# Adding the intra-chunk numerator to the inter-chunk product on TensorE instead of VectorE, in a causal linear-attention and mixture-of-experts kernel

## The chip, the cores and the metric

The kernel runs on one core of a Trainium2 chip. The metric is the device time of one execution in microseconds (us), from launch to end; the span in the profile is the shorter stretch from the first to the last instruction. The engines are named as in the profile: PE is TensorE (PEld its weight loads), DVE is VectorE, ACT is ScalarE, POOL is GpSimd, SP is SyncE. SBUF is the on-chip working memory, PSUM the memory that PE writes its products to.

## The reference

One sequence of 2048 tokens of width 128 goes through causal linear attention (16 heads of 8), a residual and a layer norm, then a top-2 mixture of 8 experts, a residual and a second layer norm. The change lies in the attention, which is, cut to what matters:

```python
q = elu(x @ Wq.T) + 1;  k = elu(x @ Wk.T) + 1;  v = x @ Wv.T     # (l, 16, 8) each
kv_cumsum = cumsum(k[..., :, None] * v[..., None, :], axis=l)
k_cumsum  = cumsum(k, axis=l)
out = einsum('lhd,lhde->lhe', q, kv_cumsum)
normalizer = clip(einsum('lhd,lhd->lh', q, k_cumsum), 1e-6, None)
x = layernorm(x + (out / normalizer[..., None]).reshape(l, 128) @ Wo.T)
```

What follows (router, softmax, top 2, two gated matrix products per expert, weighted sum, layer norm) isn't touched by the change.

## The kernel before, in words

The tokens are 16 chunks of 128, in 4 groups of 4. A chunk n (n from 0 to 15) goes through these instructions in the attention stage:

- PE projects x to q, k, v (`project`, L547). ACT makes exp and relu of q and k and copies v (`inputs`, L770 to L774). DVE forms elu + 1 of q and k in one instruction with two SBUF inputs (`features`, L952, written to `qk`). POOL forms all products k times v, with a ninth column of ones per head for the normalizer, as one SBUF instruction of 128x1152 (`outer`, L455, written to `kv`).
- PE transposes q (L555) and forms the prefix sum over the chunk's tokens as three products with a triangular matrix, one per bank (`prefix`, L560, widths 432, 432 and 288). In this document they are called the first, second and third prefix sum of the chunk.
- DVE multiplies each of the three by q (L978) and sums over d (L985) to `num`, the chunk's own numerator and normalizer, 128x144. It masks the running state of all earlier chunks for the next chunk (`mask_state`, L963).
- PE multiplies the transposed q by the masked state (`inter`, L574) to `inter_ps` in PSUM. DVE adds `num` to `inter_ps` (L994), clips the normalizer columns (`den`, L997), takes the reciprocal (L1000) and multiplies (`o`, L1004).
- PE transposes o (`turn_o`, L581), updates the state (`state`, L567), and forms the output product and residual (`put_out`, L587, L589). ACT copies on the way.

Every engine has its own queue, written out in order by a `step(g, m, ...)` function that all engines run through in the same order (`groups`); chunk n = 4g + m. Engines meet only in semaphores. DVE's `attend(n)` (called step n below) does in this order: `features` of chunk n+3, the three products of chunk n, the sum L985, `mask_state` of chunk n+1, the addition L994, `den`, the reciprocal, `o`. PE does `project` of chunk n+4, `prefix` of chunk n, `turn_o` of chunk n-1, `state` of n, `inter` of n, `put_out` of n-1; the prefix sums of chunk n+1 wait only for their PSUM bank (`pre_used`), so PE can run a chunk ahead of DVE. POOL's `outer` of chunk n+3 waits for `features` of chunk n+3.

Between these, `between(i)` interleaves on DVE the layer-norm statistics and the routing of the group before, one kind of work per step of the group (`parts`, L1185): in steps 5, 9 and 13 the variance (`mean_and_variance`, with `negm` L1045 and `vare` L1053, L1060), in steps 6, 10 and 14 the shift (`shifts_of`, L1066, at i = 3), in steps 7, 11 and 15 the choice of two experts (`choose`, at i = 3 to 8), in steps 8 and 12 the weights and places (`weigh_and_place`, at i = 2 to 7; the one for the last whole group follows after step 15). Place 4 is behind `mask_state`, place 5 ahead of `den`, place 6 behind `den`, place 7 behind the reciprocal. Many of these are additions or products of two small SBUF tiles, recorded on the helper's line L1016; one of them writes the expert weights into `rows` (`weigh_and_place`, i = 6), one forms the first indicator `ind` (`choose`, i = 5).

The choice in steps 7, 11, 15 needs the router's logits, which come by a chain that the shift starts: DVE shift, ACT normalises the four chunks (`rows`, L812), PE turns them (L594) and multiplies by the router (L601), ACT copies the logits (`lgs`, L827). The shift needs `root`, which POOL makes (L461) from the variance, ahead of its `outer` in steps 5, 9, 13. POOL also splits the expert weights (`w_lo`, L477, four pairs of instructions between steps 3 and 7) and scatters rows to DRAM (L469). The expert stage begins when the attention stage has ended.

Of the kernel before, what the change touches and what calls it, by code (L numbers as in the profile page):

```python
# [12 lines left out]
AX = mybir.AxisListType  # L13

P = 128
# [3 lines left out]
GROUP = 4  # L19
# [6 lines left out]
H, HD = 16, 8  # L26
HE = HD + 1
# [55 lines left out]
def build(nc, xT, x, wqkv, wo, rw, rscale, pes, gate_w, lin_w, consts, out):  # L83
# [4 lines left out]
    with ExitStack() as ctx:  # L88
        def sb(name, shape, dt=F32):
            return ctx.enter_context(nc.sbuf_tensor(name, shape, dt))  # L90
# [4 lines left out]
        def sem(name):  # L95
            return ctx.enter_context(nc.semaphore(name))
# [3 lines left out]
        def const(name):  # L100
            a, b = CONST[name]
            return C[:, a:b]
# [19 lines left out]
        v1 = sb("v1", [P, 2 * GROUP, H * HE])  # L122
        kv = sb("kv", [P, GROUP, KV])
        prod = sb("prod", [P, KV])
        num = sb("num", [P, H * HE])
        den = sb("den", [P, H])
        rden = sb("rden", [P, H])
        o = sb("o", [P, 2, D])
        qT = sb("qT", [P, 2, P])
        oT = sb("oT", [P, 2, P])  # L130
        state_m = sb("state_m", [P, 2, H * HE])
# [71 lines left out]
        inter_ps, rank_ps = B[6][:, 0:H * HE], B[6][:, 256:256 + (GROUP + 1) * E]  # L203
# [26 lines left out]
        state_used = sem("state_used")  # L230
        inter_done = sem("inter_done")
        state_done = sem("state_done")
        inter_used = sem("inter_used")
        o_done = sem("o_done")
        oTp_done = sem("oTp_done")
        oT_done = sem("oT_done")
# [1 line left out]
        summed = sem("summed")  # L238
# [72 lines left out]
        def exists(g, m):  # L311

            return not isinstance(g, int) or 0 <= GROUP * g + m < CHUNKS
# [18 lines left out]
        def after(eng, signal, count):  # L332

            if not (isinstance(count, int) and count <= 0):
                eng.wait_ge(signal, count)
# [206 lines left out]
        def _(pe):  # L542
# [7 lines left out]
            def prefix(g, m):  # L550

                n, s = GROUP * g + m, m % GROUP
                pe.wait_ge(phi_done, n + 1)
                after(pe, qT_done, n)
                pe.transpose(qT_ps, qk[:, s, 0:D], const("ident")).then_inc(qTp_done, 1)  # L555
                pe.wait_ge(kv_done, n + 1)
                for b, (h0, h1) in enumerate(HEADS):
                    after(pe, pre_used, 3 * (n - 1) + b + 1 if not isinstance(g, int) or n else 0)
                    c0, c1 = h0 * HE * HD, h1 * HE * HD
                    pe.matmul(pre_ps[b][:, 0:c1 - c0], const("tri"), kv[:, s, c0:c1], start=True, stop=True)\  # L560
                      .then_inc(pre_done, 1)
# [8 lines left out]
            def inter(g, m):  # L570
                n = GROUP * g + m
                pe.wait_ge(qT_done, n + 1)
                after(pe, o_done, n)
                pe.matmul(inter_ps, qT[:, m % 2, :], state_m[:, m % 2, :], start=True, stop=True)\  # L574
                  .then_inc(inter_done, 1)

            def turn_o(g, m):
                n = GROUP * g + m
                pe.wait_ge(o_done, n + 1)
                after(pe, y_used, n)  # L580
                pe.transpose(oT_ps, o[:, m % 2, :], const("ident")).then_inc(oTp_done, 1)  # L581
# [9 lines left out]
            def turn_z(g):  # L591
                pe.wait_ge(z_done, GROUP * g + GROUP)
                for i in range(GROUP):
                    t = pe.transpose(turn_ps[:, i * P:(i + 1) * P], z_of(GROUP * g + i), const("ident"))  # L594
                t.then_inc(zTp_done, 1)
# [46 lines left out]
            def step(g, m, route):  # L642
                if route == 2:
                    if exists(g, m - 1):
                        prefix(g, m - 1)
                    if exists(g, m + 3):
                        project(g, m + 3)
                    pe.wait_ge(qT_done, GROUP * g + m if exists(g, m - 1) else CHUNKS)
                    turn_z(g - 1)
                    state(g, m - 1)  # L650
                    inter(g, m - 1)
                    pe.wait_ge(y_used, GROUP * g + m - 2)
                    logits(g - 1)
                    pe.wait_ge(lgs_done, g)
                    turn_o(g, m - 2)
                    put_out(g, m - 2)
                    return
                first = isinstance(g, int) and g == 0 and m == 1
                if exists(g, m + 3) and not first:
                    project(g, m + 3)  # L660
                if isinstance(g, int) and g == 0 and m == -1:
                    clear_state()
                if exists(g, m - 1):
                    prefix(g, m - 1)
                if first:
                    project(g, m + 3)
                if exists(g, m - 2):
                    turn_o(g, m - 2)
                if exists(g, m - 1):
                    state(g, m - 1)  # L670
                if route == 3:
                    ranks(g - 1)
                elif exists(g, m - 1):
                    inter(g, m - 1)
                if exists(g, m - 2):
                    if isinstance(g, int) and g == 0 and m == 2:
                        pe.wait_ge(set_up, 5)
                        pe.wait_ge(wr_loaded, 32)
                        pe.wait_ge(x_loaded, 16)
                    put_out(g, m - 2)  # L680
                if route == 3 and exists(g, m - 1):
                    pe.wait_ge(rank_used, g)
                    inter(g, m - 1)
# [70 lines left out]
            for g in PE_PAIRS:  # L754
                c = slice(PAIR * g, PAIR * g + PAIR)
                pe.matmul(sum_ps[g], const("ident"), z_of(c),
                          start=True, stop=False)
            for g in PE_PAIRS:
                c = slice(PAIR * g, PAIR * g + PAIR)
# [166 lines left out]
        def _(ve):  # L926
# [19 lines left out]
            def features(g, m):  # L946

                n, s = GROUP * g + m, m % GROUP
                ve.wait_ge(act_in, 3 * (n + 1))
                after(ve, state_done, n - GROUP + 1)  # L950
                after(ve, kv_done, n - GROUP + 1)
                ve.scalar_tensor_tensor(out=qk[:, s, :], in0=eqk[:, m % 2, :], scalar=1.0, in1=rqk[:, m % 2, :],  # L952
                                        op0=ALU.min, op1=ALU.add).then_inc(phi_done, 1)
# [11 lines left out]
            def attend(g, m, between):  # L965


                n, s = GROUP * g + m, m % GROUP
                q = qk[:, s, 0:D].rearrange("p (h d) -> p h d", d=HD)
                if exists(g, m + 3):  # L970
                    features(g, m + 3)
                for b, (h0, h1) in enumerate(HEADS):
                    ve.wait_ge(pre_done, 3 * n + b + 1)
                    if b == 0:
                        after(ve, summed, n)
                    nh = h1 - h0
                    cols = nh * HE * HD
                    ve.tensor_tensor(  # L978
                        prod[:, h0 * HE * HD:h1 * HE * HD].rearrange("p (h e d) -> p h e d", e=HE, d=HD),
                        pre_ps[b][:, 0:cols].rearrange("p (h e d) -> p h e d", e=HE, d=HD),  # L980
                        q[:, h0:h1, :].unsqueeze(2).to_broadcast([P, nh, HE, HD]), ALU.mult).then_inc(pre_used, 1)
                    between(b)
                ve.wait_ge(pre_used, 3 * (n + 1))
                after(ve, inter_used, n)
                ve.tensor_reduce(num[:, :], prod[:, :].rearrange("p (c d) -> p c d", d=HD), AX.X,  # L985
                                 ALU.add).then_inc(summed, 1)
                between(3)
                if exists(g, m + 1):
                    mask_state(g, m + 1)
                between(4)  # L990
                ve.wait_ge(inter_done, n + 1)
                ve.wait_ge(summed, n + 1)
                after(ve, o_done, n)
                ve.tensor_tensor(inter_ps, inter_ps, num[:, :], ALU.add).then_inc(inter_used, 1)  # L994
                between(5)
                ve.wait_ge(inter_used, n + 1)
                ve.tensor_scalar(den[:, :], heads(inter_ps)[:, :, HD], DEN_MIN, None, ALU.max).then_inc(den_done, 1)  # L997
                between(6)
                ve.wait_ge(den_done, n + 1)
                ve.reciprocal(rden[:, :], den[:, :]).then_inc(rden_done, 1)  # L1000
                between(7)
                ve.wait_ge(rden_done, n + 1)
                after(ve, oTp_done, n - 1)
                ve.tensor_tensor(o[:, m % 2, :].rearrange("p (h d) -> p h d", d=HD), heads(inter_ps)[:, :, 0:HD],  # L1004
                                 rden[:, :].unsqueeze(2).to_broadcast([P, H, HD]), ALU.mult).then_inc(o_done, 1)
                between(8)
# [362 lines left out]
```

## Time and profile before

| What | us |
|---|---|
| Three runs | 217.81, 219.90, 220.21 (median 219.90) |
| The profiled execution | 217.63 |
| its span, first to last instruction | 215.8 |
| attention: first product of chunk 0 (DVE) | at 15.20 |
| first shift of the last group's chain (step 14) | at 94.69 |
| first transpose of the expert stage (PE, L702) | at 109.17 |

The times in the rows below are of the profiled execution, counted from its first instruction; 1.8 us of its 217.63 lie outside the span. A DVE row's stated duration overlaps the start of the next instruction by about 0.1 us, so costs are best read from one start to the next.

### The profile page before, as it was taken

What the parts mean: (1) busy time and instruction counts of PE and PEld (TensorE: products, weight loads), DVE (VectorE), ACT (ScalarE), POOL (GpSimd) and SP (SyncE); (2) the same over time, 40 slices, a digit from 0 to 9 for tenths busy, and PEclk for the clock granted to TensorE, in tenths of its full rate; (3) what the DMA queues carried; (4) which work ended last, traced back from release to release, by engine and by line L of the source; (5) the groups of instructions that cost most, each with busy time, mean ns of one, the idle gap of its engine ahead of it and who ended that gap; (6) DMA issues with size and microseconds to landing.
All of it is one profiled execution on the core that took longest, in us unless ns stands there. A gap on an engine that the chain in (4) does not pass through costs nothing.

```text
span 215.8 us, 3402 instructions
## 1 busy us (share of the span) xinstructions
PE 159.0 (74%) x780; PEld 115.3 (53%) x780; DVE 145.6 (67%) x517; ACT 91.7 (42%) x310; POOL 132.8 (62%) x119
## 2 busy tenths in 40 slices
PE   3698997776898589767445999940799999970540
PEld 0355664445565366445324988730688888850430
DVE  0579999999999977997346686850156666622580
ACT  2324674444236522442344555630255666610280
POOL 6585469199545987385047755677646666661570
PEclk9999999998899958997555899996589999999597
DMA  5839400000000001001410151252533311115741
GB/s 160 228 84 372 193 27 15 12 2 10 0 10 19 25 14 39 25 26 52 99 35 32 55 123 55 86 160 77 147 105 94 89 54 46 49 36 162 244 138 53
DMA packets 18626, 17.56 MB, mean 81 GB/s; under 512 B 2880, under 2 KB 16192, under 8 KB 18480
## 3 DMA queue, kind: packets, MB, share of 16 engines
q1 hardware_dynamic: 16304, 12.66, 20.4%
q0 software_dynamic: 2304, 4.69, 6.6%
q8 instruction: 7, 0.11, 0.2%
q14 instruction: 11, 0.09, 0.1%
HBM read 10.62 MB, written 6.73 MB: 80 GB/s over the span
## 4 chain that ended last, share of the span: by engine, by line
PE 41%; DVE 23%; issue 11%; DMA 8%; ACT 8%; SPq 5%; POOL 2%; DVEq 0%; POOLq 0%; ACTq 0%
PE bank L725 8%; DVE prod L978 7%; PE bank L711 4%; PE bank L712 4%; PE bank L713 4%; DVE num L985 4%; PE bank L560 4%; PE bank L733 4%; PE bank L547 4%; ACT junk L804 3%; DMA zbuf<-pads 2%; DMA pl<-both 2%; PE bank L702 2%; ACT rows L812 1%; PE bank L761 1%
## 5 line engine op out<-in xcount | busy, mean ns | idle before, releaser
L511 POOL DMA_INDIRECT both<-yout,zin x39 | 37.4, 960 | 20.4 <-DVE yout L1255 17.1
L469 POOL DMA_INDIRECT zbuf<-rows,slot x32 | 31.2, 974 | 24.7 <-DVE slot L1122 16.6
L455 POOL TENSOR_TENSOR kv<-v,qk 128x1152 f32<-128x1152 f32 x16 | 35.0, 2188 | 12.5 <-DVE qk L952 12.4
L560 PE MATMUL bank<-kv,C 128*128 128x432 f32 (+1 forms) x96 | 36.4, 518 | 0.0
L725 PEld LDWEIGHTS bank<-w_l,actT 128*128 128x128 f32 x156 | 22.4, 201 | 8.3 <-issue 7.5
L725 PE MATMUL bank<-w_l,actT 128*128 x156 | 25.8, 291 | 1.1 <-ACT actT L903 1.1
L560 PEld LDWEIGHTS bank<-kv,C 128*128 128x128 f32 x96 | 18.5, 208 | 14.6 <-issue 13.5
L978 DVE TENSOR_TENSOR prod<-bank,qk 128x432 f32<-128x432 f32 (+1 forms) x48 | 24.1, 546 | 0.9 <-PE bank L560 0.8
L1255 DVE COPY yout<-bank 128x128 f32<-128x128 f32 x39 | 11.3, 290 | 17.8 <-PE bank L725 17.7
L711 PE MATMUL bank<-w_hi,zin_hi 128*128 x39 | 20.2, 519 | 3.9 <-DVE zin_lo L1240 3.9
L898 ACT ACTIVATE gelu<-bank 128x256 f32<-128x256 f32 x39 | 15.0, 385 | 16.4 <-PE bank L713 16.4
L985 DVE TENSOR_REDUCE num<-prod 128x144 f32<-128x1152 f32 x16 | 21.6, 1352 | 0.5
L547 PE MATMUL bank<-w_qkv,xTs 128*128 128x384 f32 x32 | 16.9, 616 | 6.1 <-DMA xTs<-in_xT 3.5
L903 ACT COPY actT<-bank 128x256 f32<-128x256 f32 x39 | 14.5, 372 | 13.8 <-PE bank L733 13.8
L1240 DVE TENSOR_TENSOR zin_lo<-bank,zin_hi 128x128 fp32r<-128x128 f32 x39 | 11.2, 287 | 13.4 <-ACT zin_hi L893 11.2
L702 PE MATMUL bank<-C,zin 128*128 128x128 f32 x39 | 11.5, 299 | 11.8 <-DMA zin<-zbuf 10.0
L1248 DVE SCALAR_TENSOR_TENSOR act<-gelu,zin,bank 128x256 f32<-128x256 f32 x39 | 18.4, 471 | 0.9 <-ACT gelu L898 0.9
L712 PE MATMUL bank<-w_lo,zin_hi 128*128 x39 | 16.6, 425 | 0.0
L713 PE MATMUL bank<-w_hi,zin_lo 128*128 x39 | 16.6, 425 | 0.0
L733 PE MATMUL bank<-C,act 128*128 128x128 f32 x78 | 15.7, 285 | 0.0
L893 ACT CAST zin_hi<-bank 128x128 fp32r<-128x128 f32 x39 | 10.5, 271 | 10.7 <-PE bank L702 10.7
L952 DVE SCALAR_TENSOR_TENSOR qk<-eqk,rqk 128x256 f32<-128x256 f32 x16 | 12.0, 750 | 3.2 <-ACT v L774 3.1
(137 smaller groups left out, 315.2 us busy)
## 6 DMA issues: line engine op xcount, KB each, us to landing
zin<-zbuf SPq DMA_DIRECT2D x39, 65.0 KB, 1.9
w_g<-in_gate_w SPq DMA_DIRECT2D x4, 512.0 KB, 6.2
pl<-both SPq DMA_DIRECT2D x8, 256.0 KB, 5.3
xTs<-in_xT SPq DMA_DIRECT2D x16, 64.0 KB, 2.4
w_l<-in_lin_w SPq DMA_DIRECT2D x1, 1024.0 KB, 9.5
out<-pl SPq DMA_DIRECT2D x8, 128.0 KB, 1.8
both<-yout,zin POOLq DMA_INDIRECT x39, 2.2
zbuf<-pads SPq DMA_DIRECT2D x8, 65.0 KB
```

Source lines behind the costliest of these rows:

```text
L455: pool.tensor_tensor(kv[:, s, :].rearrange("p (h e d) -> p h e d", e=HE, d=HD), a, b, ALU.mult).then_inc(kv_done, 1)
L469: pool.indirect_dma_start(zbuf, bass.IndirectOffsetOnAxis(ap=slot[:, g, r, j:j + 1].bitcast(U32), axis=0), rows[:, GROUP * g + j, r, :], N ...
L511: pool.indirect_dma_start(both, bass.IndirectOffsetOnAxis(ap=zin[:, b, D + 1:D + 2].bitcast(U32), axis=0), yout[:, b, :], None).then_inc(p ...
L547: pe.matmul(qkv_ps[:, 0:3 * D], xTs[:, m % GROUP, :], w_qkv[:, :], start=True, stop=True)\
L560: pe.matmul(pre_ps[b][:, 0:c1 - c0], const("tri"), kv[:, s, c0:c1], start=True, stop=True)\
L711: pe.matmul(g, zin_hi[:, b % 2, :], hi, start=True, stop=False)
L712: pe.matmul(g, zin_hi[:, b % 2, :], lo, start=False, stop=False)
L713: pe.matmul(g, zin_lo[:, b % 2, :], hi, start=False, stop=True).then_inc(gate_done, 1)
L725: mm = pe.matmul(yout_ps(k), actT[:, b % 2, h, :], w_l[:, bass.ds(e * (HB * D) + h * D, D)], start=(h == 0), stop=(h == HB - 1))
L733: mm = pe.transpose(actT_ps[b % 2][:, h * P:(h + 1) * P], act[:, b % 2, h * P:(h + 1) * P], const("ident"))
L978: ve.tensor_tensor(prod[:, h0 * HE * HD:h1 * HE * HD].rearrange("p (h e d) -> p h e d", e=HE, d=HD), pre_ps[b][:, 0:cols].rearrange("p (h ...
L985: ve.tensor_reduce(num[:, :], prod[:, :].rearrange("p (c d) -> p c d", d=HD), AX.X, ALU.add).then_inc(summed, 1)
```

## The change

`num` gets two buffers. DVE no longer adds: PE leaves the product `inter` open in PSUM (`stop=False`) and closes it by a product of the identity with `num` (`join`), which waits for the sum L985 of that chunk. `join` of chunk n stands in PE's queue between the first and second prefix sum of chunk n+1 (for chunk 15 ahead of `turn_o`). DVE's `den` waits for `joined`. `features` of chunk n+3 moves in DVE's queue from the head of step n to behind `mask_state` and place 4, ahead of place 5 and `den`.

```diff
-        num = sb("num", [P, H * HE])
+        num = sb("num", [P, 2, H * HE])
...
                 for b, (h0, h1) in enumerate(HEADS):
+                    if b == 1 and exists(g, m - 1):
+                        join(g, m - 1)
                     after(pe, pre_used, 3 * (n - 1) + b + 1 if not isinstance(g, int) or n else 0)
...
-                pe.matmul(inter_ps, qT[:, m % 2, :], state_m[:, m % 2, :], start=True, stop=True)\
+                pe.matmul(inter_ps, qT[:, m % 2, :], state_m[:, m % 2, :], start=True, stop=False)\
                   .then_inc(inter_done, 1)
+
+            def join(g, m):
+                n = GROUP * g + m
+                pe.wait_ge(summed, n + 1)
+                pe.matmul(inter_ps, const("ident"), num[:, m % 2, :], start=False, stop=True).then_inc(joined, 1)
...
                 if exists(g, m - 2):
+                    if not exists(g, m - 1):
+                        join(g, m - 2)
                     turn_o(g, m - 2)
...
-                if exists(g, m + 3):
-                    features(g, m + 3)
                 for b, (h0, h1) in enumerate(HEADS):
...
-                after(ve, inter_used, n)
-                ve.tensor_reduce(num[:, :], prod[:, :].rearrange("p (c d) -> p c d", d=HD), AX.X,
+                after(ve, joined, n - 1)
+                ve.tensor_reduce(num[:, m % 2, :], prod[:, :].rearrange("p (c d) -> p c d", d=HD), AX.X,
                                  ALU.add).then_inc(summed, 1)
                 between(3)
                 if exists(g, m + 1):
                     mask_state(g, m + 1)
                 between(4)
-                ve.wait_ge(inter_done, n + 1)
-                ve.wait_ge(summed, n + 1)
+                if exists(g, m + 3):
+                    features(g, m + 3)
+                between(5)
+                ve.wait_ge(joined, n + 1)
                 after(ve, o_done, n)
-                ve.tensor_tensor(inter_ps, inter_ps, num[:, :], ALU.add).then_inc(inter_used, 1)
-                between(5)
-                ve.wait_ge(inter_used, n + 1)
                 ve.tensor_scalar(den[:, :], heads(inter_ps)[:, :, HD], DEN_MIN, None, ALU.max).then_inc(den_done, 1)
```

## Rows read from the trace of the kernel before

**Rows 1.** The page, part 1: busy time, share of the span, instructions

```profile
PE 159.0 (74%) x780; PEld 115.3 (53%) x780; DVE 145.6 (67%) x517; ACT 91.7 (42%) x310; POOL 132.8 (62%) x119
```

**Rows 2.** Busy time by stretch (length, engines with their instruction counts, PE clock): steps 0 to 6

```profile
15.20:49.50 34.30, 28.90 (x127) 18.32 (x126) 33.11 (x78) 18.25 (x67) 22.27 (x14) 1.00 0.30 103
```

**Rows 3.** Timeline of DVE, steps 1 to 3 (start, duration, instruction)

```profile
19.71 1.70 DVE L978 TENSOR_TENSOR prod<-bank,qk 128x432 f32<-128x432 f32 x3
...
24.31 1.48 DVE L978 TENSOR_TENSOR prod<-bank,qk 128x432 f32<-128x432 f32 x3
25.82 1.35 DVE L985 TENSOR_REDUCE num<-prod 128x144 f32<-128x1152 f32 x1
27.09 0.30 DVE L963 TENSOR_TENSOR state_m<-bank,C 128x144 f32<-128x144 f32 x1
27.30 0.30 DVE L994 TENSOR_TENSOR bank<-bank,num 128x144 f32<-128x144 f32 x1
27.64 0.17 DVE L997 TENSOR_SCALAR den<-bank 128x16 f32<-128x16 f32 x1
...
28.35 0.41 DVE L952 SCALAR_TENSOR_TENSOR qk<-eqk,rqk 128x256 f32<-128x256 f32 x1
28.77 1.49 DVE L978 TENSOR_TENSOR prod<-bank,qk 128x432 f32<-128x432 f32 x3
```

**Rows 4.** Timeline of PE: prefix sums of chunks 1 and 12, and one plain step

```profile
18.78 2.10 PE L560 MATMUL bank<-kv,C 128*128 128x432 f32 x6
...
24.65 0.27 PE L581 MATMUL bank<-C,o 128*128 128x128 f32 x1
...
28.52 0.29 PE L581 MATMUL bank<-C,o 128*128 128x128 f32 x1
28.65 0.41 PE L567 MATMUL bank<-v,qk 128*128 128x144 f32 x2
...
79.28 3.93 PE L560 MATMUL bank<-kv,C 128*128 128x432 f32 x6
```

**Rows 5.** Timeline of POOL: the products of chunks 6, 10 and 12

```profile
28.84 2.18 POOL L455 TENSOR_TENSOR kv<-v,qk 128x1152 f32<-128x1152 f32 x1 [2.20 <-DVE qk L952]
...
54.02 2.17 POOL L455 TENSOR_TENSOR kv<-v,qk 128x1152 f32<-128x1152 f32 x1
...
69.42 2.16 POOL L455 TENSOR_TENSOR kv<-v,qk 128x1152 f32<-128x1152 f32 x1
```

**Rows 6.** Timeline of DVE: small instructions with two SBUF inputs, steps 7, 10, 14

```profile
54.45 1.79 DVE L1016 TENSOR_TENSOR ind<-C,r_k 128x32 f32<-128x32 f32 x1
...
71.01 0.60 DVE L1066 TENSOR_TENSOR shift<-negm,root 128x4 f32<-128x4 f32 x1
...
94.69 0.15 DVE L1066 TENSOR_TENSOR shift<-negm,root 128x4 f32<-128x4 f32 x1
```

**Rows 7.** Timeline of DVE: steps 8, 11 and 12

```profile
58.22 1.48 DVE L978 TENSOR_TENSOR prod<-bank,qk 128x432 f32<-128x432 f32 x3
...
61.82 0.30 DVE L994 TENSOR_TENSOR bank<-bank,num 128x144 f32<-128x144 f32 x1
...
62.25 0.16 DVE L1016 TENSOR_TENSOR rows<-w,pe_of 128x8 f32<-128x8 f32 x1
...
63.37 1.11 DVE L978 TENSOR_TENSOR prod<-bank,qk 128x432 f32<-128x432 f32 x2
...
77.20 0.18 DVE L1025 TENSOR_REDUCE r_m<-lgs 128x4 f32<-128x32 f32 x1 [1.22 <-ACT lgs L827]
...
84.15 0.23 DVE L1016 TENSOR_TENSOR pos<-bank,ind 128x64 f32<-128x64 f32 x1 [0.45 <-PE bank L630]
...
86.37 0.31 DVE L994 TENSOR_TENSOR bank<-bank,num 128x144 f32<-128x144 f32 x1
...
86.81 0.16 DVE L1016 TENSOR_TENSOR rows<-w,pe_of 128x8 f32<-128x8 f32 x1
...
87.42 1.11 DVE L978 TENSOR_TENSOR prod<-bank,qk 128x432 f32<-128x432 f32 x2
```

More of the change, by code:

```diff
@@ L232, in build @@
         state_done = sem("state_done")
-        inter_used = sem("inter_used")
+        joined = sem("joined")
         o_done = sem("o_done")
```

## The prediction

> **What bounds the kernel now.** I read the busy times of the page first. No engine is full over the whole span: PE 159.0 us, DVE 145.6, POOL 132.8 of 215.8 [rows 1], so the bound has to be found by stage. The busy times by stretch show it: in the 34.30 us of steps 0 to 6 DVE is busy for 33.11 us and PE for 28.90, at a granted clock of 1.00, which is the upper of PE's two levels [rows 2]. DVE sets the pace of the attention stage. The timeline of DVE gives the price of a plain step from one first product to the next: 28.77 - 24.31 = 4.46 us [rows 3]. The timeline of PE gives 28.52 - 24.65 = 3.87 us where PE doesn't wait [rows 4]: it has 0.59 us to spare in a step.
>
> In the steps with routing work DVE is held by other things too, and those decide here. The shift of step 10 took 0.60 us and the same instruction in step 14 took 0.15 [rows 6]. The long one ended at 71.61; POOL's products of chunk 12 ran until 69.42 + 2.16 = 71.58 [rows 5]. The first indicator of step 7 began at 54.45 and ended at 56.24 [rows 6], and POOL's products of chunk 10 ended at 54.02 + 2.17 = 56.19 [rows 5]. Both DVE instructions have two SBUF inputs and both end just as POOL's instruction does. The chunk products L978, which take one input from PSUM, ran at 1.49 us for three at 28.77 while POOL worked from 28.84 on [rows 3, 5], as they do at 24.31 with 1.48. So a DVE instruction with two SBUF inputs waits out a POOL product that is under way, and one with a PSUM input doesn't.
>
> **The change part by part.** I keep a ledger of how much later than before a place of the kernel comes (minus is earlier). The sum is made against the profiled execution, 217.63 us: span 215.8 and 1.8 around it.
>
> *The addition goes, the join comes.* The addition costs DVE 27.64 - 27.30 = 0.34 us a step [rows 3]. The join is not in the trace. Its nearest row is the state update, two passes of the same 128x144: 0.41 us [rows 4]. At PE's lower clock level I scale by the prefix sums, 3.93 against 2.10 us for the same six instructions [rows 4]: 0.77 us. So its bounds are 0 (hidden) and 0.77; I take 0.41, the row of its own shape. A handover between engines costs 0.08: features at 28.35 end at 28.76, POOL begins at 28.84 [rows 3, 5]. The sum L985 ends at 25.82 + 1.35 = 27.17, so the join is done at 27.17 + 0.08 + 0.41 + 0.08 = 27.74. Meanwhile DVE does the mask from 27.09 (0.21) and the moved features (28.77 - 28.35 = 0.42): to 27.72. The join is hidden, with nothing to spare; I allow 0.1. A plain step falls from 4.46 to 4.46 - 0.34 + 0.1 = 4.22. PE needs up to 3.87 + 0.41 = 4.28: it becomes as tight as DVE. Behind the waiting join stand the second and third prefix sums, `turn_o`, the state, `inter`; DVE needs the second prefix sum only after den, reciprocal, o and one product, about 1.2 us behind the join, and the prefix sum takes 0.79 us (below). That wait costs nothing while the clock is up.
>
> *The start.* The join of chunk 0 stands behind the first prefix sum of chunk 1, which begins at 18.78 [rows 4]; with 432/1152 of 2.10 = 0.79 for that it is done at 18.78 + 0.79 + 0.41 = 19.98. Den, reciprocal and o take 28.77 - 27.64 - 0.42 = 0.71, so chunk 1's product begins at 20.7 instead of 19.71 [rows 3]: 1.0 later. Six steps at 0.24 give 1.4 back. Ledger at chunk 7: **-0.4** (bounds -0.5 and +0.9, the latter if features meet both halves of a weight split on POOL).
>
> *Features moved.* The instruction itself costs the same, 0.42. It releases three things: ACT's next `inputs`, PE's transpose and POOL's products of chunk n+3. The first prefix sum that needs those products comes two steps later, so lateness costs nothing there. No DMA is issued or passed. But POOL's 2.18 us of products now start 0.49 after features [rows 3, 5] and so lie behind `mask_state`, over places 5 to 8, where before they lay over the chunk products and the sum, which they don't hold. In plain steps nothing with two SBUF inputs follows. In steps 5, 9, 13 POOL is held by `roots`. In steps 7, 8, 11, 12 small instructions with two SBUF inputs follow.
>
> *Step 7.* Its logits come at the old time, since their chain hangs on the variance of step 5, where +0.42 and -0.34 cancel. Before, the indicator waited until 56.24. Now features run just ahead of it. POOL is in the weight split until about 54.02 [rows 5], now some 0.4 later; then a key instruction (0.2) and features follow, and POOL's products run from 54.02 + 0.4 + 0.2 + 0.49 = 55.1 to 57.3. The indicator, or the two-input instructions right behind den, wait for that: 1.1 later, less the 0.35 of features no longer at the end of the step. Ledger at chunk 8: **+0.8** (bounds +0.4, +1.2).
>
> *Step 8.* Features stand where the addition stood, 61.82 + 0.8 = 62.62 [rows 7]. POOL's products go from 63.11 to 65.29. The write of the weights into `rows` would be due at 62.25 + 0.8 + 0.1 = 63.15 [rows 7], just behind POOL's start, and it waits until 65.29. From there to the next product is 87.42 - 86.81 = 0.61 (step 12, which had no features behind it) [rows 7]: chunk 9 at 65.90 against 63.37. Ledger: **+2.5**. The margin of this race is small (0.04, some 0.1 more if den waits for the join), so the bounds are +0.4 (it slips through) and +2.6.
>
> *Steps 9 to 11.* Step 9 gains 0.34 and gives 0.1 back, but its variance comes 0.1 later still, and with it root, POOL's products of chunk 12, the shift, and the logits: +2.6 at 77.20 [rows 7]. PE then does the first prefix sum of chunk 12 at its lower clock (3.93 for six, from 79.28 [rows 4]) and the join behind it delays the rest. The ranks that step 12 waits for at 84.15 [rows 7] come **+2.8** later (bounds +2.3 with the clock up, +3.2).
>
> *Step 12.* The same as step 8: features at 86.37 + 2.8 = 89.17, POOL from 89.66 to 91.84, the write of the weights due at 89.7 waits to 91.84, chunk 13 at 92.45 against 87.42 [rows 7]: **+5.0**.
>
> *Steps 13 and 14* have no features left and gain 0.34 each, less 0.1 for the join: **+4.6** at the shift of step 14. From there the chain by ACT, PE and the logits to the expert stage is untouched (the join of chunk 15 falls into a wait for ACT), and the expert stage hangs on it whole. Sum: 217.63 + 4.6 = 222.2 in an execution like the profiled one. That one lies 2.3 below the median of the runs shown, 219.90, from which the sum is 224.5. I give 223.5, the nearer to the median since a later median is asked.
>
> **A rule weighed.** The traced waits of 0.60 and 1.79 us [rows 6] could be chance neighbours of POOL's ends. The Trainium skill, SBUF — State Buffer, "Who interferes with whom", says that a VectorE instruction with two SBUF inputs and a GpSimd instruction that reads SBUF exclude each other: whoever comes first holds the shared port for its whole instruction. By that rule steps 8 and 12 lose what I set down; without it the sum is that of the second rival. This trace agrees where it shows the case, with POOL first; who wins when both come within 0.1 us no row here shows.
>
> **The rivals.**
> 1. *One race won, one lost.* Step 12's write slips through and step 8's doesn't, or the other way round: 4.6 - 2.2 = +2.4, 222.3 from the median. For it: margins of 0.1 us.
> 2. *Not slower: both writes get ahead of POOL.* The place is `rows` behind den, the price 2.2 each, and it decides at the moment when POOL's products start reading, 0.49 after features or somewhat later than their recorded start. Then the ledger is +0.8 at chunk 8, +0.4 at chunk 9, about +1.0 at chunk 13 and +0.6 at the end: 220.5, within 1%. Against it: den waits for the join, which pushes the write further behind POOL.
> 3. *Slower still by the clock.* PE now stands idle behind the held o of chunks 8 and 12 for 1.5 us each; if its clock falls to the lower level there, the next six prefix sums cost 3.93 - 2.10 = 1.8 more on a PE without slack, twice: +8.2, 228.1. For it: the slow prefix sums at 79.28 follow waits of PE. Against: in steps 0 to 6 the clock stayed at 1.00 through shorter waits [rows 2].
> 4. *Faster.* If neither POOL nor the logit chains mattered, 15 steps at 0.24 less the start's 1.0 give -2.6: 217.3. Against it: the shift and logit chains are paced by POOL, ACT and PE, not by the addition.
>
> **How the numbers follow.** Forecast 0.60; rivals 1 to 4: 0.12, 0.18, 0.06, 0.04. A measurement of this kernel tells about 1% (2.2 us) from no change. Slower by over 1%: 0.60 + 0.06 and half of rival 1, with a little of rival 2's upper end, 0.74. Faster by over 1%: 0.04. Within 1%: 0.22. The range: rival 2 from an execution like the profiled one is 218.2, and the forecast's upper bounds (+1.0) from the median are 225.5; to leave out no more than 2 in 10 it goes from 218.5 to 227.0.
>
> **What would show it.** Right: in steps 8 and 12 the write into `rows` (L1016) lasts about 2 us and ends with POOL's L455; chunk 9's first product comes about 2.5 us late, chunk 13's 5; plain steps are near 4.2; den follows features at once. Wrong: `rows` instructions of 0.16 us in both steps, plain steps not below 4.46, long waits of den for the join, or prefix sums of 3.9 us in steps where they took 2.1.

## The result, and the profile after

The changed kernel is slower: 221.97 us against 218.37 (medians of 18 runs each), a ratio of 1.0128 with a 95% interval of 1.0096 to 1.0159, or 2.8 us with 2.1 to 3.5. The medians lie 3.6 us apart; the ratio and its interval are taken over the fast runs alone, without slow ones such as one of 238.69 us. The forecast was 223.5 us, 4.6 more than before, in a range of 218.5 to 227.0.

The page of the changed kernel, part 1, answers to [rows 1]. PE has 32 instructions more (16 joins of two passes), DVE 16 fewer (the additions):

```profile
PE 162.6 (75%) x812; PEld 115.9 (53%) x812; DVE 146.7 (67%) x501; ACT 92.0 (42%) x310; POOL 133.0 (61%) x119
```

DVE lost 16 additions of 0.32 us, yet its busy time rose from 145.6 to 146.7 us. A wait for POOL counts as busy time of the waiting DVE instruction, so the loss already shows in this line.

The busy times by stretch, for the plain steps of the changed kernel (columns as in [rows 2]): PE is now busier than DVE, 32.07 of 35.00 us, at the upper clock level.

```profile
15.00:50.00 35.00, 32.07 (x141) 20.20 (x139) 31.46 (x70) 18.41 (x66) 21.87 (x13) 1.00 0.30 101
```

The timeline of DVE in the changed kernel: the start and a plain step (answering to [rows 3]), then steps 5, 7, 8, 11 and 12 (answering to [rows 6, 7]). L985 are the chunk products, L992 the sum, L961 features, L1003 den, L1022 the helper's line, L1051 `negm`.

```profile
20.84 0.17 DVE L1003 TENSOR_SCALAR den<-bank 128x16 f32<-128x16 f32 x1 [1.57 <-PE bank L582]
...
25.72 1.47 DVE L985 TENSOR_TENSOR prod<-bank,qk 128x432 f32<-128x432 f32 x3
...
28.71 0.41 DVE L961 SCALAR_TENSOR_TENSOR qk<-eqk,rqk 128x256 f32<-128x256 f32 x1
29.18 0.17 DVE L1003 TENSOR_SCALAR den<-bank 128x16 f32<-128x16 f32 x1
...
29.89 1.47 DVE L985 TENSOR_TENSOR prod<-bank,qk 128x432 f32<-128x432 f32 x3
...
39.94 0.64 DVE L1051 TENSOR_SCALAR negm<-ysum 128x4 f32<-128x4 f32 x1
...
55.48 2.17 DVE L1022 TENSOR_TENSOR ind<-C,r_k 128x32 f32<-128x32 f32 x1
57.90 0.17 DVE L1003 TENSOR_SCALAR den<-bank 128x16 f32<-128x16 f32 x1 [0.25 <-PE bank L582]
...
63.18 0.41 DVE L961 SCALAR_TENSOR_TENSOR qk<-eqk,rqk 128x256 f32<-128x256 f32 x1
63.51 0.15 DVE L1022 TENSOR_TENSOR w<-w,r_elog 128x4 f32<-128x4 f32 x1
63.72 0.17 DVE L1003 TENSOR_SCALAR den<-bank 128x16 f32<-128x16 f32 x1
63.81 2.06 DVE L1022 TENSOR_TENSOR rows<-w,pe_of 128x8 f32<-128x8 f32 x1
...
66.28 1.11 DVE L985 TENSOR_TENSOR prod<-bank,qk 128x432 f32<-128x432 f32 x2
...
81.05 2.17 DVE L1022 TENSOR_TENSOR ind<-C,r_k 128x32 f32<-128x32 f32 x1
...
89.08 2.18 DVE L1022 TENSOR_TENSOR rows<-w,pe_of 128x8 f32<-128x8 f32 x1
...
91.66 1.11 DVE L985 TENSOR_TENSOR prod<-bank,qk 128x432 f32<-128x432 f32 x2
```

The timeline of POOL for the same places, products of chunks 7, 10, 11, 14 and 15:

```profile
38.38 2.18 POOL L455 TENSOR_TENSOR kv<-v,qk 128x1152 f32<-128x1152 f32 x1 [0.36 <-DVE qk L961]
...
55.42 2.17 POOL L455 TENSOR_TENSOR kv<-v,qk 128x1152 f32<-128x1152 f32 x1 [0.46 <-DVE qk L961]
...
63.67 2.17 POOL L455 TENSOR_TENSOR kv<-v,qk 128x1152 f32<-128x1152 f32 x1 [6.08 <-DVE qk L961]
...
81.00 2.17 POOL L455 TENSOR_TENSOR kv<-v,qk 128x1152 f32<-128x1152 f32 x1 [1.74 <-DVE qk L961]
...
89.06 2.17 POOL L455 TENSOR_TENSOR kv<-v,qk 128x1152 f32<-128x1152 f32 x1 [0.94 <-DVE qk L961]
```

Read the two together. In step 8 features end at 63.59, POOL starts at 63.67 and ends at 65.84, and the write into `rows`, 0.16 us in [rows 7], begins at 63.81 and ends at 65.87. In step 12 it is 91.23 for POOL and 91.26 for the write. In step 11, where the kernel before had an indicator of 0.19 us at 79.06, it begins 0.05 behind POOL and takes 2.17. The instruction `w` at 63.51, also with two SBUF inputs, came 0.16 before POOL and took 0.15. The plain step is 29.89 - 25.72 = 4.17 us, den following features with no gap.

The timeline of PE: a plain join, and the held turns of o behind steps 8 and 12 with the prefix sums after them (answering to [rows 4]; L562 is the prefix sum, L582 the join, L588 the turn of o).

```profile
27.95 0.89 PE L562 MATMUL bank<-kv,C 128*128 128x432 f32 x2
28.68 0.46 PE L582 MATMUL bank<-num,C 128*128 128x144 f32 x2
...
66.41 0.33 PE L588 MATMUL bank<-C,o 128*128 128x128 f32 x1 [1.52 <-DVE o L1010]
...
68.40 0.89 PE L562 MATMUL bank<-kv,C 128*128 128x432 f32 x2
...
82.54 0.69 PE L582 MATMUL bank<-num,C 128*128 128x144 f32 x2
...
91.80 0.33 PE L588 MATMUL bank<-C,o 128*128 128x128 f32 x1 [1.99 <-DVE o L1010]
...
93.14 0.89 PE L562 MATMUL bank<-kv,C 128*128 128x432 f32 x2
```

PE stood idle for 1.52 and 1.99 us, and the first prefix sum behind each took 0.89 us, as in the plain step; the granted clock is 1.00 from 66.4 to 70.0 and from 91.8 to 95.5. The join at 82.54 ran at a granted clock of 0.50, the lower level.

The ledger of the prediction, place by place, in this pair of profiled executions (starts in us):

| Place | before | after | forecast | measured |
|---|---|---|---|---|
| product of chunk 1 | 19.71 | 21.54 | +1.0 | +1.8 |
| product of chunk 7 | 49.49 | 49.86 | -0.4 | +0.4 |
| product of chunk 8 | 58.22 | 59.58 | +0.8 | +1.4 |
| product of chunk 9 | 63.37 | 66.28 | +2.5 | +2.9 |
| logits in step 11 | 77.20 | 79.86 | +2.6 | +2.7 |
| ranks in step 12 | 84.15 | 86.36 | +2.8 | +2.2 |
| product of chunk 13 | 87.42 | 91.66 | +5.0 | +4.2 |
| shift of step 14 | 94.69 | 98.76 | +4.6 | +4.1 |
| expert stage, first transpose | 109.17 | 112.82 | +4.6 | +3.7 |

### The profile page after: what moved, and what is told of

It reads as the page before. It is cut to its first block, busy times and chain, and to the rows that moved or that the text cites. A ratio compares the mean times of both kernels' runs of the same rounds, so it can differ in the third digit from the quotient of the medians.

```text
span 218.2 us, 3448 instructions
## 1 busy us (share of the span) xinstructions
PE 162.6 (75%) x812; PEld 115.9 (53%) x812; DVE 146.7 (67%) x501; ACT 92.0 (42%) x310; POOL 133.0 (61%) x119
## 4 chain that ended last, share of the span: by engine, by line
PE 47%; DVE 15%; issue 10%; ACT 9%; DMA 8%; SPq 5%; POOL 3%; POOLq 0%; DVEq 0%; ACTq 0%
PE bank L734 8%; PE bank L562 7%; PE bank L547 5%; PE bank L720 4%; PE bank L721 4%; PE bank L722 4%; DVE prod L985 4%; PE bank L742 4%; ACT junk L813 3%; DMA zbuf<-pads 2%; DMA pl<-both 2%; ACT rows L821 2%; DVE rows L1022 2%; PE bank L711 2%; PE bank L594 2%
## 5 line engine op out<-in xcount | busy, mean ns | idle before, releaser
L562 PE MATMUL bank<-kv,C 128*128 128x432 f32 (+1 forms) x96 | 40.0, 531 | 0.0
L734 PEld LDWEIGHTS bank<-w_l,actT 128*128 128x128 f32 x156 | 21.5, 195 | 8.2 <-issue 7.4
L985 DVE TENSOR_TENSOR prod<-bank,qk 128x432 f32<-128x432 f32 (+1 forms) x48 | 24.0, 547 | 2.8 <-PE bank L562 2.7
L734 PE MATMUL bank<-w_l,actT 128*128 x156 | 25.0, 283 | 1.1 <-ACT actT L912 1.1
L562 PEld LDWEIGHTS bank<-kv,C 128*128 128x128 f32 x96 | 17.6, 209 | 9.4 <-issue 9.0
L992 DVE TENSOR_REDUCE num<-prod 128x144 f32<-128x1152 f32 x16 | 21.6, 1353 | 0.5
L779 ACT ACTIVATE eqk<-bank 128x256 f32<-128x256 f32 x16 | 6.1, 384 | 17.5 <-PE bank L547 13.4
```

The source lines that it names most:

```text
L734: mm = pe.matmul(yout_ps(k), actT[:, b % 2, h, :], w_l[:, bass.ds(e * (HB * D) + h * D, D)], start=(h == 0), stop=(h == HB - 1))
L985: ve.tensor_tensor(prod[:, h0 * HE * HD:h1 * HE * HD].rearrange("p (h e d) -> p h e d", e=HE, d=HD), pre_ps[b][:, 0:cols].rearrange("p (h ...
L992: ve.tensor_reduce(num[:, m % 2, :], prod[:, :].rearrange("p (c d) -> p c d", d=HD), AX.X, ALU.add).then_inc(summed, 1)
```

## The experiments

Theory A: the moved features release POOL's products into a stretch of DVE instructions that wait for them. Rival B: the join's wait and a PE without slack cost the time.

**Features back at the head of the step, the join kept** (changed kernel)

```diff
+                if exists(g, m + 3):
+                    features(g, m + 3)
                 for b, (h0, h1) in enumerate(HEADS):
...
                 between(4)
-                if exists(g, m + 3):
-                    features(g, m + 3)
                 between(5)
```

> The changed kernel with the features instruction back at the head of the step; the join stays. Theory A (POOL's products, released by the moved features, hold the two-input writes of steps 8 and 12): the writes into rows take 0.16 us again, the 2.1 and 2.2 us are gone, but nothing but the mask covers the join, so a plain step is 4.46 - 0.34 + 0.4 = about 4.5 us and the start still loses over 1 us; ratio to before between 0.995 and 1.006. Rival B (the join's wait and a PE without slack cost the time, wherever features stand): the writes don't matter, the ratio stays at 1.010 to 1.016 or rises.

Measured: ratio 1.0039, interval 1.0001 to 1.0077. The timeline of DVE of this kernel, den of chunk 7 and the write of step 8:

```profile
59.94 0.17 DVE L1003 TENSOR_SCALAR den<-bank 128x16 f32<-128x16 f32 x1 [1.42 <-PE bank L582]
...
66.19 0.16 DVE L1022 TENSOR_TENSOR rows<-w,pe_of 128x8 f32<-128x8 f32 x1
```

The write is short again and 0.9% of the time is gone, though the join is where it was: the move of features, not the join, carries most of the loss. The plain step is 4.51 us (sums at 28.14 and 32.65), so a join that only the mask covers gives back what the addition cost. B has a part: den of chunk 7 waits 1.42 us for PE.

**The move of features alone** (kernel before)

```diff
-                if exists(g, m + 3):
-                    features(g, m + 3)
                 for b, (h0, h1) in enumerate(HEADS):
...
                 between(4)
+                if exists(g, m + 3):
+                    features(g, m + 3)
                 ve.wait_ge(inter_done, n + 1)
```

> The kernel before with features moved behind the mask and place 4; the addition stays on DVE and there is no join. Theory A: the writes into rows of steps 8 and 12 take about 2 us each, plain steps stay at 4.46, steps 1 to 6 give back nothing; ratio 1.012 to 1.020. Rival B: no join, no loss: 0.997 to 1.004.

Measured: ratio 1.0181, interval 1.0123 to 1.0240. The timeline of DVE in step 8, and below it that of POOL:

```profile
63.37 0.41 DVE L952 SCALAR_TENSOR_TENSOR qk<-eqk,rqk 128x256 f32<-128x256 f32 x1
63.70 0.31 DVE L994 TENSOR_TENSOR bank<-bank,num 128x144 f32<-128x144 f32 x1
63.92 2.13 DVE L1016 TENSOR_TENSOR w<-w,r_elog 128x4 f32<-128x4 f32 x1
65.98 0.16 DVE L997 TENSOR_SCALAR den<-bank 128x16 f32<-128x16 f32 x1
66.09 0.17 DVE L1016 TENSOR_TENSOR rows<-w,pe_of 128x8 f32<-128x8 f32 x1
```

```profile
63.87 2.17 POOL L455 TENSOR_TENSOR kv<-v,qk 128x1152 f32<-128x1152 f32 x1 [5.77 <-DVE qk L952]
```

With no join at all the kernel loses no less than by the whole change (the intervals overlap, so more isn't shown). The victim is the instruction one earlier: the addition stands between, so `w` comes 0.05 us behind POOL's start and waits 2 us, and the write behind it, expected to be the long one, is free. The plain step was 4.37 us, not 4.46. In this trace something came on top that the changed kernel hadn't: behind the held o of steps 8 and 12 the granted clock fell to 0.50 (68.25 to 71.66 and 92.14 to 95.55), as rival 3 of the prediction has it. The timeline of PE shows the prefix sums there, 3.27 us instead of 2.10, so part of the 1.8% can be the clock:

```profile
69.32 3.27 PE L560 MATMUL bank<-kv,C 128*128 128x432 f32 x6
```

**The two weight instructions ahead of features** (changed kernel)

```diff
                 if i == 4:
...
-                if i == 5:
                     tt(w12[:, 1], w12[:, 0], A["elog"], ALU.mult, last=1)
-                if i == 6:
                     tt(rows[...
```

> The changed kernel with the two two-input instructions of the weights (places 5 and 6) done at place 4, ahead of features; everything else as in the changed kernel, join and place of features included. Theory A: nothing with two SBUF inputs is left behind features in steps 8 and 12, so 4.2 us go, less some 0.1: 217.5 to 218.5 where the changed kernel has 222, ratio 0.992 to 0.998. Rival B: 1.010 to 1.016 as in the changed kernel.

Measured: ratio 1.0008, interval 0.9966 to 1.0050: two small instructions done 0.3 to 0.4 us sooner take away the slowdown, with the join and the features where the change put them. The size was missed: 1.2% is 2.6 us, not 4.2. The timeline of DVE from step 8 into step 9, and of POOL:

```profile
63.12 0.17 DVE L1022 TENSOR_TENSOR rows<-w,pe_of 128x8 f32<-128x8 f32 x1
63.23 0.42 DVE L961 SCALAR_TENSOR_TENSOR qk<-eqk,rqk 128x256 f32<-128x256 f32 x1
...
63.77 0.25 DVE L1006 RECIPROCAL rden<-den 128x16 f32<-128x16 f32 x1
63.94 0.16 DVE L1126 TENSOR_REDUCE slot<-pos 128x8 int32<-128x64 f32 x1
64.06 0.29 DVE L1010 TENSOR_TENSOR o<-bank,rden 128x128 f32<-128x128 f32 x1
64.27 1.11 DVE L985 TENSOR_TENSOR prod<-bank,qk 128x432 f32<-128x432 f32 x2
65.30 0.64 DVE L1051 TENSOR_SCALAR negm<-ysum 128x4 f32<-128x4 f32 x1
```

```profile
63.73 2.18 POOL L455 TENSOR_TENSOR kv<-v,qk 128x1152 f32<-128x1152 f32 x1 [6.36 <-DVE qk L961]
```

Reciprocal, reduction and the two instructions with a PSUM input run beside POOL at their own length. `negm`, with a single SBUF input, waits until POOL ends at 65.91: the queue moved forward and the next victim took half a microsecond, in step 9 and again in step 13. It starts the chain of the variance, so that counts. By the traces this accounts for the size: the two steps had lost 1.5 and 2.0 us, not 4.2 together, and `negm` takes back 0.5 twice.

**Features behind o in steps 7, 8, 11, 12, joins of chunks 0, 7 and 11 early** (changed kernel)

```diff
-                    if b == 1 and exists(g, m - 1):
+                    if b == 1 and exists(g, m - 1) and not early(n - 1):
...
+            def early(n):
+                return isinstance(n, int) and n in (0, 7, 11)
...
                     pe.wait_ge(lgs_done, g)
+                    if early(GROUP * g + m - 1):
+                        join(g, m - 1)
...
                     inter(g, m - 1)
+                    if GROUP * g + m - 1 == 0:
+                        join(g, m - 1)
...
-                if exists(g, m + 3):
+                if exists(g, m + 3) and not late:
                     features(g, m + 3)
...
                 between(8)
+                if exists(g, m + 3) and late:
+                    features(g, m + 3)
...
-                    attend(g, m - 1, between)
+                    attend(g, m - 1, between, route in (2, 3))
```

> The changed kernel with features behind o in the steps that choose and weigh (7, 8, 11, 12) and behind place 4 in the others, and with the join of chunk 0 right behind its inter-chunk product and those of chunks 7 and 11 ahead of the turn of o, instead of between the prefix sums of the next chunk. Theory A: no long rows write, no 2.17 us indicator from POOL's products of the same step, den of chunk 0 some 1.5 us sooner; plain steps 4.18; ratio 0.978 to 0.992, a gain over both kernels. Rival B: PE without slack still sets the pace; ratio 1.000 to 1.010.

Measured: ratio 1.0011, interval 0.9965 to 1.0057. By the number alone B had it, though the twelve runs spread from 216.10 to 221.35 us. The timeline of DVE shows a loss that isn't B's, `negm` of steps 9 and 13:

```profile
63.44 1.33 DVE L1060 TENSOR_SCALAR negm<-ysum 128x4 f32<-128x4 f32 x1
...
87.65 2.17 DVE L1060 TENSOR_SCALAR negm<-ysum 128x4 f32<-128x4 f32 x1
```

The products of chunks 11 and 15 now start at 62.57 and 87.60, over `negm` of the next step.

**The same, with negm of steps 9 and 13 ahead of those features**

```diff
-                if i == 1:
+                if i == 1 and g == 0:
                     mean(g, 0, GROUP)
...
                 between(8)
+                if isinstance(g, int) and g in (1, 2) and m == GROUP:
+                    mean(g, 0, GROUP)
                 if exists(g, m + 3) and late:
```

> The kernel with early joins (chunks 0, 7, 11) and features behind o in steps 7, 8, 11, 12, in which negm of steps 9 and 13 is done at the end of steps 8 and 12, ahead of those features. Theory A, widened by the runs before (one-input instructions on SBUF such as negm wait for POOL's products too: 1.33 and 2.17 us there): negm takes 0.15 to 0.2 us again, the sums of chunks 9 and 13 come 1.2 and 2.0 us sooner than with early joins alone, and the shift of step 14 about 3; ratio to before 0.982 to 0.993. Rival B (PE without slack sets the pace): 1.000, as with early joins alone.

Measured: ratio 0.9962, interval 0.9926 to 0.9999. `negm` takes 0.16 us in both places, and from the sum of chunk 8 to that of chunk 9 it is 65.81 - 60.78 = 5.03 us instead of 65.17 - 58.96 = 6.21, from 12 to 13 4.59 instead of 6.60: the 1.2 and 2.0 us expected. The gain as a whole fell short of the expected ratio, and the shift of step 14 came 1.4 us sooner (95.15 against 96.57), not 3; 0.5 of the rest is the first prefix sums, 4.04 us against 3.57. Its timeline of PE shows the prefix sums of chunk 8, and the line below, from that of DVE, the product that waited (in this version L992 is a chunk product):

```profile
56.63 2.86 PE L562 MATMUL bank<-kv,C 128*128 128x432 f32 x6
```

```profile
58.31 1.70 DVE L992 TENSOR_TENSOR prod<-bank,qk 128x432 f32<-128x432 f32 x3 [0.43 <-PE bank L562]
```

The same six took 2.10 us at 55.13 in the version before it, at a granted clock of 1.00; here it is 0.73 over the 2.86 us. With POOL out of the way, the product waits 0.43 us for PE, which runs partly at its lower level, and that of chunk 12 waits 0.76: there B has a part. This version has the lowest ratio of all, 1.6% under the changed kernel (0.9962 / 1.0127) and just under the kernel before.

**The same without the early joins**

```diff
-                return isinstance(n, int) and n in (0, 7, 11)
+                return isinstance(n, int) and n in ()
...
-                    if GROUP * g + m - 1 == 0:
+                    if early(GROUP * g + m - 1):
```

> As the kernel with early joins and negm ahead of features, but with every join between the first and second prefix sum of the next chunk, as in the change. Theory A: den of chunk 0 comes 1.5 us later again, den of chunks 7 and 11 wait for PE for 1 to 2 us each, for nothing but the join; ratio 0.995 to 1.006. Rival B: as with early joins, since PE's work is the same.

Measured: ratio 1.0044, interval 0.9995 to 1.0093, as expected. What the place of three joins is worth isn't settled by the times: the ratios lie 0.8% apart, but the intervals touch and the twelve runs here spread from 217.98 to 223.69 us. The traces show where it goes: from the start of chunk 0's sum to its den it is 20.14 - 16.71 = 3.43 us here and 19.73 - 17.64 = 2.09 with the join early, and den of chunks 7 and 11 waits 2.18 and 2.08 us for PE, where it didn't wait with the joins early. The timeline of DVE, den of chunk 7:

```profile
56.95 0.17 DVE L1010 TENSOR_SCALAR den<-bank 128x16 f32<-128x16 f32 x1 [2.18 <-PE bank L582]
```

The indicator ahead of it took 0.19 us in this trace, and step 7 still 58.98 - 49.19 = 9.79 us, against 8.07 with the joins early and 9.72 in the changed kernel: in that step the late join alone is enough for the delay.

**The changed kernel again**, unedited:

> The changed kernel as it is, once more, on the chip and in the rounds of the others. All theories: ratio 1.010 to 1.016; rows in steps 8 and 12 again about 2.1 us; the first three prefix sums take between 2.9 and 4.0 us by the moment at which the clock rises.

Measured: ratio 1.0127, interval 1.0072 to 1.0182. The writes took 2.07 and 2.18 us, the six first prefix sums 3.48, and the expert stage began at 112.98.

**The kernel before again, twice**, unedited, one profiled execution each:

> The kernel before, unchanged, looked at again to see how much of the distance between the two traces is the moment at which PE's clock rises. In the first trace the six prefix-sum instructions of chunk 0 took 2.92 us, in six traces of other versions 3.5 to 4.0. Theory: here they take 3.3 to 4.0 and the shift of step 14 comes 0.3 to 0.8 later than the 94.69 of the first trace, so that the changed kernel's distance there shrinks from 4.07 to some 3.5 us. Rival: the six take 2.9 in the kernel before whenever it runs, and the later rise belongs to the change.

> The same kernel once more, as a second draw of the same moment: between 2.9 and 4.0 us for the six, the shift of step 14 between 94.7 and 95.6.

The timelines of PE of the two, first prefix sums and first transpose of the expert stage:

```profile
13.15 3.53 PE L560 MATMUL bank<-kv,C 128*128 128x432 f32 x6
...
111.71 0.66 PE L702 MATMUL bank<-C,zin 128*128 128x128 f32 x2 [1.78 <-DVE base L1107]
```

```profile
13.08 3.12 PE L560 MATMUL bank<-kv,C 128*128 128x432 f32 x6
...
109.48 0.66 PE L702 MATMUL bank<-C,zin 128*128 128x128 f32 x2 [1.87 <-DVE base L1107]
```

The shift of step 14 came at 96.79 and 94.94 (expected 95.0 to 95.5, and 94.7 to 95.6; the first went past it). The records of the granted clock begin with the upper level, at 14.69 us in the first trace of the kernel before, at 16.02 and 15.12 in these two and at 16.48 in the changed kernel; the six instructions took 2.92, 3.53, 3.12 and 3.82 us. The later rise isn't the change's: 3.53 and 3.12 us lie among the 3.08 to 4.04 of the other versions, and the 2.92 of the first trace was the shortest of all traces. Only 0.7 of the 2.1 us of the first of the two is the start (chunk 1's product at 20.43 against 19.71). In steps 7 and 8 its granted clock was 0.50 from 50.2 to 60.4 us, in the first trace only from 52.2 to 55.7, and chunk 9's product came 2.4 us late. The expert stage began at 109.17, 111.71 and 109.48 in three traces of the kernel before, mean 110.12, and at 112.82 and 112.98 in two of the changed one, mean 112.90: 2.8 us, as the runs measured. So close a match is partly luck, since from there to the end the five executions took between 105.4 and 107.6 us.

## Why the prediction was right

The direction, the mechanism and its two places hold. Point by point:

- *Addition and join.* Forecast 4.22 us for a plain step, measured 4.17. The join took 0.46 us behind a prefix sum (forecast 0.41) and was hidden; at the lower clock level 0.69 (upper bound 0.77). Without features as its cover the step is 4.51: the cover is worth 0.34.
- *The start.* Forecast +1.0, measured +1.8. Of this, 0.9 is the first prefix sums of chunk 0, 3.82 us against 2.92, which differ from execution to execution. Steps 1 to 6 gave back 1.5 (forecast 1.4).
- *Step 7.* Forecast +1.2, measured +1.0, and two causes ended within 0.3 us of each other: the indicator's wait for POOL ended at 57.65, the join let den go at 57.90. The prediction had the indicator alone there; the kernel without the early joins shows that the late join holds the step by itself.
- *Steps 8 and 12.* Forecast +1.7 and +2.2, measured +1.5 and +2.0. The open question, who wins a race of 0.1 us, is answered: 0.05 us behind POOL's recorded start (the move alone) and 0.02 (step 12) are enough to lose, 0.16 ahead enough to win. Moving the two instructions ahead of features took the loss away with the join in place, so the cause of these two losses is shown, not argued.
- *Steps 9 to 12's ranks.* Forecast +0.3 from chunk 9 to the ranks, measured -0.7. This is the term with the wrong sign. It left out that the indicator of step 11 now waits for POOL too (2.17 us against 0.19), so that chunk 12's product comes 3.7 late. And it added the join at PE's lower clock, though more fell away: the wait of 0.97 us that the key instruction `r_eq` had in the kernel before (0.18 now), and DVE's waits of 0.58, 0.24 and 0.45 for PE in step 12, which are gone now that DVE itself comes later.
- *The sum.* Forecast 4.6, measured 2.8. In this pair of traces the shift is 4.1 late, the expert stage 3.7: 0.5 of the miss lies in the terms above, 0.4 in the chain behind the shift, which was set down as untouched and took 14.06 us instead of 14.48 (14.92 and 14.54 in the two later traces of the kernel before, 14.33 in the second of the changed one). The last 0.9 is the draw of the trace that I summed against: it began the expert stage 0.95 earlier than the mean of three. The step that failed is the base: one execution's clock was taken for the kernel's. That 217.63 + 4.6 = 222.2 lies so near the measured 221.97 is luck, since the base was 0.7 under the median of 18 runs, 218.37, and the sum too large; the 223.5 leaned on a median of three runs, 219.90, that was 1.5 above it.

The rows of the kernel before that the term of the ranks left out (timeline of DVE):

```profile
77.52 0.97 DVE L1016 TENSOR_TENSOR r_eq<-lgs,r_m 128x32 f32<-128x32 f32 x1
...
82.40 0.61 DVE L978 TENSOR_TENSOR prod<-bank,qk 128x432 f32<-128x432 f32 x1 [0.58 <-PE bank L560]
83.24 0.46 DVE L978 TENSOR_TENSOR prod<-bank,qk 128x288 f32<-128x288 f32 x1 [0.24 <-PE bank L560]
```

What a DVE instruction waits for was put too narrowly. I gave two SBUF inputs as the condition; `negm`, with one, took 0.64 us at 39.94 and ended at 40.58, as POOL's products of chunk 7 did at 38.38 + 2.18 = 40.56; so POOL isn't held in step 5 as the prediction has it. Two experiments missed their size by this (0.64 twice, 1.33 and 2.17 us). The Trainium skill, SBUF — State Buffer, "Who interferes with whom", counts `tensor_scalar` among the operations that can contend with GpSimd for the shared port, by a mode of their own that uses both ports. This trace agrees as to the wait; the mode no run shows.

The rivals: neither write got ahead of POOL (rivals 1 and 2). The clock didn't fall behind the held turns of o (rival 3): 0.89 us for the first prefix sum after waits of 1.52 and 1.99. In the kernel with the move alone it did (granted clock 0.50), so this rival was nearer than one pair of traces shows. No gain came through (rival 4).

## What to carry to other kernels

An instruction that is moved takes along what it releases: before features are moved to fill a wait, look at what the released engine will run next and which DVE instructions will then lie beside it. By these traces, DVE products, sums and scalings that read only SBUF, even 8 elements long, belong ahead of such a release or more than its 2.2 us behind it; those with a PSUM input, and reductions and reciprocals, can lie beside it. And a sum made against one trace needs a second and third trace of the same kernel where its clock moves.

## What was not expected of the hardware

PE's clock rises to its upper level at a moment that differs by execution: between 14.69 and 17.19 us in the clock records of eleven traces, where the same six instructions from 13.0 to 13.2 us on took 2.92 to 4.04 us. A DVE instruction that waits for POOL is recorded as busy, 2.06 us for 8 elements, so a share of busy time can rise when work is taken away.
